# One-hot table reads: seven tables in the first half and ten in every later one, and a new order for the last tile, on one Trainium2 core

## The chip, the cores and the metric

The kernel runs on 1 core of one Trainium2 chip. The metric is the device time of one execution in microseconds; before the change the median of three runs is 620.69 us (620.36 to 627.76).

## The reference, cut to what matters

A batch of 2048 rows looks up 27 embedding tables of width 128, takes all pairwise dot products of the 27 rows of one sample, appends 16 dense features, and puts the 367 values through a small tower of layers.

```python
e = jnp.stack([tbl_f[ids[:, f]] for f in range(27)], axis=1)   # (2048, 27, 128); tables of 1000, 1250, 12500, 125000 rows
dot = jnp.einsum('bnd,bmd->bnm', e, e)
z = dot.reshape(2048, 27 * 27)[:, lower_triangle]              # 351 pairs
h = jnp.concatenate([z, dense_ctx], axis=1)                    # 367
h = jnp.maximum(h @ W_top1 + b_top1, 0.0)                      # 512
h = jnp.maximum(h @ W_top2 + b_top2, 0.0)                      # 256
y = h @ W_top3                                                 # 1
```

## The kernel before, in words

The batch is cut into 16 tiles (`t`) of 128 samples; two tiles make a half (`h`, eight of them). Every sample's 27 embedding rows must stand transposed in `embT` (the width of 128 on partitions). They get there in two ways.

**Gathered tables.** POOL issues one indirect DMA per table and tile (L324); it puts 128 rows of 512 bytes into `emb`, which holds two tiles. TensorE transposes them four at a time (a `quad`, L365), ScalarE copies the result to `embT` (L562). POOL may gather quad q of tile t+2 only when TensorE has transposed quad q of tile t (semaphore `turned`).

**Tables read by one-hot columns.** The small tables of `ONE_HOT` (1000 rows, 8 chunks of 125, or 1250 rows, 10 chunks) live in SBUF. VectorE builds a 125x256 one-hot block per chunk and half (`build`, L477), and TensorE multiplies the chunk by it (`read_table`): L355 with the table split in two parts, so two matmuls per chunk and 16 or 20 per read, or L350 on the unsplit table in the first half for tables 5 and up (8 per read; the trace has two records for each such plain fp32 matmul). ScalarE copies the result for both tiles at once (L554). Blocks are passed on in groups of two: TensorE waits for `hot_built`, and counts the used ones in `hot_used`, on which VectorE's builds (six groups ahead at most) and ScalarE's copies wait. Before the change, even halves read 9 tables so and gather 18 per tile; odd halves read 10 and gather 17.

**The rest of a tile.** `dots` (L381) makes the dot products of one tile in two steps of 64 small fp32 matmuls (128 records each), called first and second step here. VectorE transposes the result into `flat`, ScalarE picks the ring of pairs (`ring`, L570), TensorE transposes it (`flat`, L393) into `flatT`, and `layer1` (L410) and `layer2` (L434) follow one to three tiles later.

**What sets the order.** `plan(t)` writes the steps out by hand; each engine walks the same `ORDER`. In tile t it is: quad 0, first dots step of t-1, flat of t-2, a read; quad 1, a layer, a read; quad 2, second dots step, a layer, a read; quads 3 and 4, each with a read. The reads made during odd t are the first part of the next half's tables, those during even t the second part. Where only four reads fall to a tile (t = 3, 7, 11), the first place, between the first dots step and quad 1, has none. `END` holds what follows the last tile's quads. SyncE loads tables, ids and weights in program order (from L265); some tables are first put into space that a later tensor will use (`raw`).

## Time and profile before

| | |
|---|---|
| runs | 620.69 us median (620.36, 620.69, 627.76) |
| profiled execution | 628.72 us, span 626.9 us |
| TensorE busy, records | 423.8 us, 6065; mean granted clock 0.781 |
| VectorE busy | 246.2 us |
| ScalarE busy | 165.0 us |
| POOL busy (280 gathers) | 283.5 us |
| chain that ended last | PE 61%, issue 24%, unknown queue 8% |

The profiled execution is as long as the longest of the three runs, 8 us over the median. The span is what the trace covers; 1.8 us of the execution lie around it. Busy time of TensorE counts overlapping matmuls, so its share is not a share of its peak. POOL's gathers show how long it took to issue each, not when the rows landed. "remote" or "an unknown queue" in a wait means that what released it was not found beside a recorded instruction.

### The profile page before, as it was taken

The page shows a single profiled execution, that of the slowest core. Times are in us where ns is not written, and L with a number is a line of the kernel's source. Part 1 is how long each engine was busy: PE and PEld are TensorE (multiplying, and loading weights), DVE is VectorE, ACT ScalarE, POOL GpSimd, SP SyncE. Part 2 cuts the span into 40 slices and gives each one's busy share as a digit, 9 for nine tenths or more (in the row PEclk, how much of TensorE's full clock was granted, in tenths as well). Part 3 has the DMA queues.
Part 4 walks back from the last instruction along what each step waited for, and adds up shares of the span by engine and source line. Part 5 has one row for each costly group of instructions (what it writes and reads, how often), then busy time and mean ns, then how long its engine had stood idle before and what let it go on. Part 6 is the DMA issues. An engine that isn't in the chain of part 4 may idle for free.

```text
span 626.9 us, 13933 instructions
## 1 busy us (share of the span) xinstructions
PE 423.8 (68%) x6065; PEld 369.4 (59%) x6065; DVE 246.2 (39%) x760; ACT 165.0 (26%) x216; POOL 283.5 (45%) x288
## 2 busy tenths in 40 slices
PE   3206965656785693866578768486757777758997
PEld 3106765546675592855457657276645666638985
DVE  6107625527061361523416234162422524326622
ACT  2102232323222141221222213233121321214441
POOL 6774644544533476343643438534354533743000
PEclk9556966678776796777788669587767976959999
DMA  8932421514111122111212112111121211211000
GB/s 202 237 94 54 98 58 35 138 43 114 48 37 47 45 57 51 39 47 39 68 44 50 36 36 67 48 46 46 37 58 43 59 42 29 63 44 30 3 3 3
DMA packets 22924, 36.65 MB, mean 58 GB/s; under 512 B 6240, under 2 KB 17008, under 8 KB 22864
## 3 DMA queue, kind: packets, MB, share of 16 engines
q0 software_dynamic: 8960, 18.37, 11.8%
q1 hardware_dynamic: 13904, 17.39, 11.3%
q8 instruction: 48, 0.79, 0.5%
q14 instruction: 12, 0.10, 0.1%
HBM read 35.73 MB, written 0.01 MB: 57 GB/s over the span
## 4 chain that ended last, share of the span: by engine, by line
PE 61%; issue 24%; another core or an unknown queue 8%; ACT 3%; DVE 3%; DMA 1%; SPq 0%; ACTq 0%; DVEq 0%
PE embT_ps L355 23%; PE gram_ps L381 15%; PE h_ps L410 9%; PE h_ps L434 6%; PE embT_ps L365 4%; PE embT_ps L350 2%; PE flat_ps L393 2%; DVE one_hot L477 1%; ACT embT L554 1%; DVE tbl L462 1%; ACT embT L562 1%; DMA embT<-in_tbl 1%; ACT pairs L570 1%; ACT flatT L574 0%
## 5 line engine op out<-in xcount | busy, mean ns | idle before, releaser
L324 POOL DMA_INDIRECT emb<-in_tbl,idx x280 | 282.7, 1010 | 289.9 <-PE embT_ps L365 186.8
L477 DVE TENSOR_SCALAR one_hot<-ids,row_of 125x256 fp32r<-125x256 int32 x648 | 194.4, 368 | 204.7 <-PE embT_ps L355 119.9
L355 PE MATMUL embT_ps<-one_hot,tbl 125*128 125x256 f32 x1232 | 189.7, 312 | 45.0 <-issue 29.7
L355 PEld LDWEIGHTS embT_ps<-one_hot,tbl 125*128 125x128 f32 x1232 | 173.7, 213 | 50.3 <-issue 40.6
L381 PE MATMUL gram_ps<-embT 128*27 128x27 f32 x4096 | 98.7, 210 | 146.8 <-issue 128.9
L381 PEld LDWEIGHTS gram_ps<-embT 128*27 128x27 f32 x4096 | 71.2, 121 | 176.8 <-issue 156.9
L554 ACT COPY embT<-embT_ps 128x256 f32<-128x256 f32 x76 | 51.6, 682 | 278.7 <-PE embT_ps L355 176.1
L562 ACT COPY embT<-embT_ps 128x512 f32<-128x512 f32 (+2 forms) x80 | 88.6, 1110 | 11.5 <-remote 8.8
L508 DVE STREAM_TRANSPOSE flat<-gram_ps 128x864 f32<-128x864 f32 x16 | 17.3, 1083 | 123.1 <-PE gram_ps L381 123.1
L410 PE MATMUL h_ps<-flatT,w_sb 126*128 126x256 f32 (+1 forms) x192 | 56.0, 454 | 2.6 <-ACT flatT L574 2.5
L365 PE MATMUL embT_ps<-ident,emb 128*128 128x128 f32 x280 | 48.5, 293 | 3.6 <-issue 3.6
L410 PEld LDWEIGHTS h_ps<-flatT,w_sb 126*128 126x128 f32 x192 | 43.1, 242 | 11.6 <-ACT flatT L574 3.4
L365 PEld LDWEIGHTS embT_ps<-ident,emb 128*128 128x128 f32 x280 | 36.8, 152 | 4.9 <-issue 4.4
L434 PE MATMUL h_ps<-w_sb,h1T 128*128 128x256 f32 x128 | 39.3, 461 | 0.4 <-ACT h1T L594 0.2
L434 PEld LDWEIGHTS h_ps<-w_sb,h1T 128*128 128x128 f32 x128 | 28.4, 234 | 5.7 <-ACT h1T L594 0.5
L594 ACT ACTIVATE h1T<-h_ps 128x512 f32<-128x512 f32 x14 | 8.5, 607 | 81.5 <-PE h_ps L410 73.3
L574 ACT COPY flatT<-flat_ps 126x384 f32<-126x384 f32 x16 | 7.8, 485 | 58.9 <-PE flat_ps L393 52.4
L496 DVE TENSOR_TENSOR h<-h_ps,b_sb 128x256 f32<-128x256 f32 x16 | 6.8, 425 | 39.2 <-PE h_ps L434 39.2
L570 ACT COPY pairs<-flat 128x351 f32<-128x351 f32 x16 | 13.0, 813 | 2.7 <-DVE flat L509 2.7
L393 PE MATMUL flat_ps<-ident,pairs 128*126 128x128 f32 x48 | 11.9, 372 | 0.9 <-ACT pairs L570 0.9
L542 ACT CAST tbl<-embT 125x1024 fp32r<-125x1024 f32 (+1 forms) x5 | 5.7, 1133 | 15.1 <-DMA embT<-in_tbl 13.1
L509 DVE STREAM_TRANSPOSE flat<-gram_ps 128x416 f32<-128x416 f32 x16 | 9.2, 574 | 0.0
(39 smaller groups left out, 73.8 us busy)
## 6 DMA issues: line engine op xcount, KB each, us to landing
ids<-in_ids_hot SPq DMA_DIRECT2D x76, 128.0 KB
emb<-in_tbl,idx POOLq DMA_INDIRECT x280
embT<-in_tbl SPq DMA_DIRECT2D x3, 448.0 KB
embT<-in_tbl SPq DMA_DIRECT2D x2, 560.0 KB
w_sb<-in_tbl SPq DMA_DIRECT2D x2, 448.0 KB
w_sb<-in_W_ring SPq DMA_DIRECT2D x1, 756.0 KB
w_sb<-in_tbl SPq DMA_DIRECT2D x1, 560.0 KB
w_sb<-in_W_top SPq DMA_DIRECT2D x1, 512.0 KB
```

The source lines that it names most:

```text
L324: pool.indirect_dma_start(emb[:, t % EB, s, :], None, tables[f][:, :], bass.IndirectOffsetOnAxis(ap=idx[:, t, f:f + 1], axis=0),).then_inc ...
L355: mm = pe.matmul(out[:, 0:HN], tbl[0:ROWS, part, AT[o] + chunk, :], one_hot[0:ROWS, k % SLOTS, c, :], start=(chunk == 0 and part == 0), st ...
L365: mm = pe.transpose(out[:, i * P:(i + 1) * P], emb[:, t % EB, s, :], ident[:, :])
L381: mm = pe.matmul(gram_ps[32 * j:32 * j + FEATS, b, at * FEATS:(at + 1) * FEATS], rows, rows, start=True, stop=True)
L393: mm = pe.transpose(flat_ps[0:KR, k * TILE:(k + 1) * TILE], rows[:, k * KR:(k + 1) * KR], ident[:, :])
L410: mm = pe.matmul(h1_ps[:, i * width:(i + 1) * width], w1_sb[0:KR, k, c * P:(c + 1) * P], x[:, k, :], start=(k == 0), stop=(k == KC - 1))
L434: mm = pe.matmul(h2_ps[:, :], h1T[:, k, t % HT * TILE:(t % HT + 1) * TILE], w2_sb[:, k, :], start=(k == 0), stop=(k == C1 - 1))
L477: done = dve.tensor_scalar(one_hot[0:ROWS, k % SLOTS, c, :], of, row_of[0:ROWS, KINDS.index(CH[o]), chunk:chunk + 1], None, ALU.is_equal)
L508: dve.transpose(flat[:, 0:FEATS, :], by_column(0, FEATS)).then_inc(flat_filled, 1)
L554: act.copy(embT_feats[:, at:at + HT, slot(o), :], embT_ps[USE["hot", h, o] % BANKS][:, 0:HN].rearrange("p (t c) -> p t c", t=HT),).then_in ...
L562: act.copy(embT_feats[:, t % TB, s[0]:s[0] + n, :], embT_ps[USE["quad", t, q] % BANKS][:, 0:n * P].rearrange("p (f c) -> p f c", f=n),).th ...
L570: act.copy(pairs[:, t % 2, :, 1:HALF + 1], ring()).then_inc(pairs_ready, 1)
```

## The change

The one-hot tables are ordered so that the seven with 8 chunks come first. The first half (tiles 0 and 1) reads only those seven and gathers 20 tables per tile; all seven later halves read ten and gather 17. The three more rows gathered in tiles 0 and 1 than `emb` now has room for (17 per tile) land in `flatT`. The staging places of the unsplit tables and the order of SyncE's loads change with it: the last two tables are loaded in turn into `w1_sb` after the previous one there is split, and `flat` is no staging place any more. The last tile gets an order of its own. Counted over the program: 77 reads for 76, 1284 split matmuls for 1232, 16 unsplit for 32, 278 gathers for 280.

```diff
-ONE_HOT = (4, 13, 5, 6, 18, 19, 21, 22, 23, 8)
+ONE_HOT = (4, 13, 18, 19, 21, 22, 23, 5, 6, 8)
+READ_IN_HALF = (7, 10, 10, 10, 10, 10, 10, 10)
...
-    GF = FEATS - O
+    GF = FEATS - max(READ_IN_HALF)
...
     def hots_of(h):
-        return range(O if h % 2 else O - 1)
+        return range(READ_IN_HALF[h])
 
     def slot(o):
-        return GF if o == O - 1 else GF + 1 + o
+        return FEATS - 1 - o
...
         if t == T - 1:
-            after[QUADS - 2] += [("layer2", t - 3), ("ring", t - 1), ("flat", t - 1)]
-            after[QUADS - 1] += [("layer2", t - 2)]
+            return [("flat", t - 2), *dots[0], ("layer1", t - 3), ("quad", t, 0), *dots[2], ("layer1", t - 2),
+                    ("quad", t, 1), ("layer2", t - 3), ("quad", t, 2), ("ring", t - 1), ("flat", t - 1),
+                    ("layer2", t - 2), ("quad", t, 3), ("layer1", t - 1), ("quad", t, 4)]
...
-    END = [("dots", T - 1, 0, GROUPS32 // 2), ("layer1", T - 2), ("dots", T - 1, GROUPS32 // 2, GROUPS32),
-           ("layer2", T - 2), ("ring", T - 1), ("flat", T - 1), ("layer1", T - 1), ("layer2", T - 1)]
+    END = [("dots", T - 1, 0, GROUPS32), ("layer2", T - 2), ("ring", T - 1), ("flat", T - 1), ("layer1", T - 1),
+           ("layer2", T - 1)]
...
-    SPLIT_AT = {len(HOT0) + 1 + i: WHOLE + i for i in range(O - 1 - WHOLE)}
-    SPLIT_AT[len(HOT0) + O - 3] = O - 1
+    SHARED = WHOLE + 2
+    SPLIT_AT = {len(HOT0) + at: WHOLE + i for i, at in enumerate((0, 1, 2, 4, 6))}
...
-        emb = sb("emb", [P, EB, GF + 1, D])
+        emb = sb("emb", [P, EB, GF, D])
...
+        def gathered_row(t, s):
+            if s >= GF:
+                return flatT[:, s - GF, t * D:(t + 1) * D]
+            return emb[:, t % EB, s, :]
...
-                home = (flat, h1T, w2_sb, w1_sb, w1_sb)[o - WHOLE]
+                home = (h1T, w2_sb, w1_sb, w1_sb, w1_sb)[o - WHOLE]
...
-            for o in range(O - 1):
+            for o in range(SHARED + 1):
                 load_table(o)
-                load_ids(o)
+                if o < len(HOT0):
+                    load_ids(o)
...
             for n in range(EARLY, len(HOTS)):
                 load_ids(n)
-                if n == EARLY + 2:
-                    load_table(O - 1)
+                if n == EARLY:
+                    load_table(SHARED + 1)
+                elif n == EARLY + 2:
+                    load_table(SHARED + 2)
+                    sp.wait_ge(hot_used, BEFORE[len(HOT0)])
                     sp.dma_start(w2_sb[:, :, :], w2.rearrange("(k p) n -> p k n", p=P)).then_inc(weights_loaded, 16)
-                elif n == EARLY + 6:
+                elif n == EARLY + 5:
                     sp.wait_ge(low_ready, O)
                     sp.dma_start(w1_sb[0:KR, :, :], w1).then_inc(weights_loaded, 16)
...
                 dve.wait_ge(dotted, t + 1)
                 if t > 0:
                     dve.wait_ge(pairs_ready, t)
-                else:
-                    dve.wait_ge(low_ready, WHOLE + 1)
```

**TensorE's queue at the start** (line numbers moved: L355, L350, L365, L381 are L371, L366, L381, L397 after the change). Before, from the first read to the first dots step:

```order
L355 MATMUL embT_ps<-one_hot,tbl 128x256 x52
L365 MATMUL embT_ps<-ident,emb 128x128 x4
L355 MATMUL embT_ps<-one_hot,tbl 128x256 x20
...
L350 MATMUL embT_ps<-one_hot,w_sb 128x256 x16
L365 MATMUL embT_ps<-ident,emb 128x128 x6
L381 MATMUL gram_ps<-embT 27x27 x64
```

and now:

```order
L371 MATMUL embT_ps<-one_hot,tbl 128x256 x32
L381 MATMUL embT_ps<-ident,emb 128x128 x4
L371 MATMUL embT_ps<-one_hot,tbl 128x256 x16
...
L366 MATMUL embT_ps<-one_hot,w_sb 128x256 x8
L381 MATMUL embT_ps<-ident,emb 128x128
L381 MATMUL embT_ps<-ident,flatT 128x128 x3
L381 MATMUL embT_ps<-ident,emb 128x128 x4
L397 MATMUL gram_ps<-embT 27x27 x64
```

The first quad now stands after two reads, not three; two unsplit reads stand ahead of the first dots step, not four.

**TensorE's queue in tile 3**, from the first dots step to the second one, before:

```order
L381 MATMUL gram_ps<-embT 27x27 x64
L393 MATMUL flat_ps<-ident,pairs 126x128 x3
L365 MATMUL embT_ps<-ident,emb 128x128 x4
L410 MATMUL h_ps<-flatT,w_sb 128x256 x6
L355 MATMUL embT_ps<-one_hot,tbl 128x256 x16
L365 MATMUL embT_ps<-ident,emb 128x128 x4
```

and now:

```order
L397 MATMUL gram_ps<-embT 27x27 x64
L409 MATMUL flat_ps<-ident,pairs 126x128 x3
L371 MATMUL embT_ps<-one_hot,tbl 128x256 x16
L381 MATMUL embT_ps<-ident,emb 128x128 x4
L426 MATMUL h_ps<-flatT,w_sb 128x256 x6
L371 MATMUL embT_ps<-one_hot,tbl 128x256 x16
L381 MATMUL embT_ps<-ident,emb 128x128 x4
```

A read of 16 matmuls has come between the first dots step and quad 1. The same happens in tiles 7 and 11.

## Rows read from the trace of the kernel before

**Rows 1.** The page: each engine's busy time, share of the span, instructions.

```profile
PE 423.8 (68%) x6065; PEld 369.4 (59%) x6065; DVE 246.2 (39%) x760; ACT 165.0 (26%) x216; POOL 283.5 (45%) x288
```

**Rows 2.** Waits: engine line <- what it waited for: us in total, times, longest.

```profile
POOL emb L324 <- PE embT_ps L365: 186.8, 29, 10.9
PE gram_ps L381 <- issue: 128.9, 205, 1.9
ACT embT L554 <- remote: 87.7, 13, 30.3
PE embT_ps L365 <- issue: 3.6, 5, 1.6
```

**Rows 3.** Windows around single dots steps: length, busy us (instructions), clock, DMA.

```profile
461.10:467.30 6.20, 3.44 (x129) 2.42 (x129) 0.00 (x0) 1.62 (x2) 3.32 (x4) 0.50 0.16 42
494.30:504.90 10.60, 4.20 (x130) 2.77 (x129) 1.96 (x6) 2.31 (x3) 5.66 (x6) 0.75 0.24 63
227.00:228.20 1.20, 1.19 (x128) 1.16 (x128) 0.99 (x4) 1.20 (x2) 1.20 (x1) 1.00 0.15 44
583.80:585.00 1.20, 1.20 (x130) 1.13 (x128) 0.81 (x4) 1.20 (x2) 0.00 (x0) 1.00 0.00 0
```

**Rows 4.** Timeline, 0 to 54 us: start, us, engine line, [idle before <-releaser].

```profile
2.79 1.10 POOL L324 DMA_INDIRECT emb<-in_tbl,idx  x1 [1.15 <-DMA idx<-in_idx_rows]
12.43 2.63 PE L355 MATMUL embT_ps<-one_hot,tbl 125*128 125x256 f32 x16 [0.33 <-issue]
...
46.81 0.95 POOL L324 DMA_INDIRECT emb<-in_tbl,idx  x1 [0.30 <-issue]
47.99 0.61 DVE L477 TENSOR_SCALAR one_hot<-ids,row_of 125x256 fp32r<-125x256 int32 x2 [10.58 <-remote]
...
53.60 1.18 ACT L554 COPY embT<-embT_ps 128x256 f32<-128x256 f32 x2 [30.26 <-remote]
54.19 0.94 POOL L324 DMA_INDIRECT emb<-in_tbl,idx  x1 [6.44 <-remote]
```

**Rows 5.** Timeline, 54 to 86 us.

```profile
69.23 7.07 PE L350 MATMUL embT_ps<-one_hot,w_sb 125*128 125x256 f32 x32
...
83.25 0.94 POOL L324 DMA_INDIRECT emb<-in_tbl,idx  x1 [0.30 <-issue]
...
85.35 0.98 PE L381 MATMUL gram_ps<-embT 128*27 128x27 f32 x61 [1.14 <-issue]
```

**Rows 6.** Windows, tiles 7 to 10, each from its quad 0 to the next.

```profile
302.60:340.50 37.90, 25.77 (x374) 22.33 (x373) 13.34 (x42) 9.70 (x13) 17.17 (x19) 0.77 0.19 48
340.50:379.80 39.30, 27.72 (x376) 23.98 (x374) 14.78 (x51) 9.52 (x13) 17.18 (x15) 0.74 0.17 43
379.80:419.10 39.30, 27.25 (x391) 23.62 (x390) 14.73 (x47) 10.49 (x14) 21.01 (x21) 0.78 0.20 52
419.10:456.20 37.10, 26.19 (x378) 22.35 (x377) 15.23 (x49) 9.04 (x12) 16.21 (x18) 0.82 0.19 48
```

**Rows 7.** Timeline, TensorE: the read between first dots step and quad 1.

```profile
505.42 3.76 PE L355 MATMUL embT_ps<-one_hot,tbl 125*128 125x256 f32 x16
508.98 1.06 PE L365 MATMUL embT_ps<-ident,emb 128*128 128x128 f32 x4
...
228.51 2.16 PE L355 MATMUL embT_ps<-one_hot,tbl 125*128 125x256 f32 x16
230.51 0.60 PE L365 MATMUL embT_ps<-ident,emb 128*128 128x128 f32 x4
```

**Rows 8.** Timeline at 220 us, and POOL's gathers in the view by line (min/median/max).

```profile
220.55 7.45 DVE L477 TENSOR_SCALAR one_hot<-ids,row_of 125x256 fp32r<-125x256 int32 x28
222.42 6.39 POOL L324 DMA_INDIRECT emb<-in_tbl,idx  x1 [9.24 <-PE embT_ps L365]
...
L324 POOL DMA_INDIRECT emb<-in_tbl,idx x280: 938/944/6390, 2.8 to 573.3; - x140
```

**Rows 9.** Windows, quad 0 of tile 15 to the end.

```profile
594.00:626.90 32.90, 27.45 (x642) 22.97 (x640) 7.00 (x19) 11.24 (x17) 0.00 (x0) 0.99 0.01 3
```

## What the change is expected to do

> **What bounds the kernel now.** I read the page first: TensorE is busy for 423.8 us of 626.9 and no engine is full [rows 1], so the bound is a chain between engines. The waits come next [rows 2]. TensorE hardly ever waits for gathered rows (3.6 us before the transposes), but POOL waits 186.8 us for the transposes that free its buffers. The largest idle time of TensorE, 128.9 us in 205 pieces, lies inside the dots steps and has no releaser ("issue"). So I looked at single dots steps [rows 3]. All have the same 128 records. Where POOL issues nothing, at 583.8, a step takes 1.2 us; with about five gathers it takes 6.2 us, with about seven 10.6 us. The step at 227.0 tells the two causes apart that one could think of: POOL is counted busy there, but by one gather that is itself stuck (below), and the step takes 1.2 us. TensorE is therefore held while gathers are being issued, and let go some 2.8 us after the last one starts (83.25 to 86.1 in [rows 5]; the last record of that step starts within the row at 85.35).
>
> The same is seen, much larger, at the start [rows 4]. POOL issues the 36 gathers of tiles 0 and 1 without a pause, from 2.79 to 46.81, 1.25 us apart (0.94 busy and 0.30 idle). The 16 matmuls of the second table begin at 12.43, yet ScalarE's copy that waits for them starts at 53.60, and VectorE's builds that wait for `hot_used` come ten microseconds apart. All are released together 5.8 us after POOL's last gather of the burst ends (47.76), and POOL itself goes on at 54.19.
>
> So I read the kernel as turns. TensorE passes quads, which lets POOL gather 4 to 10 rows in one burst; the next dots step ends 2.8 us after that burst; only then does TensorE go on to the quad that starts the next burst. There are two such turns in a tile of 37 to 39 us [rows 6]. Two things are on the path: each gather, at 1.25 us, and what TensorE does between the end of a dots step and the next quad. Reads elsewhere lie beside the gathers. The last 32.9 us have no gather [rows 9].
>
> **The Trainium skill against this.** The rows show dots steps of 6 to 10 us beside gathers and 1.2 us without. The Trainium skill, page "SBUF — State Buffer", section "Who interferes with whom", says that TensorE and ScalarE never wait for anyone at SBUF. By that page alone the gathers would cost TensorE nothing; what follows from it is the first rival.
>
> **The change, part by part** (against the profiled execution, 628.72 us).
>
> *1. Four more gathers in tiles 0 and 1, three fewer reads there.* The first burst is 40 gathers for 36: its last one starts at 46.81 + 4 x 1.25 = 51.8, and by the same lag the release moves from 53.60 to 58.6 and POOL's restart from 54.19 to 59.2 [rows 4]. Before the first dots step can end, POOL issues 21 more (17 of tile 2, 4 of tile 3). Before, these took from 54.19 to 83.25, 29.1 us, of which 20 x 1.25 = 25.0 are gathers and 4.1 are pauses in which POOL waited for quads. TensorE has less to do in this stretch now: two of four unsplit reads go, each a half of the 7.07 us that the last two took [rows 5]. That can take away pauses, no more. The last gather then starts between 59.2 + 25.0 = 84.2 and 88.3, for 83.25: +1.0 to +5.1. I take +2.0, near the lower end, since the quads now come sooner after one another. The lower bound, if the hold is not tied to the gathers, is -7.1 (the two reads). Both ends are kept for the range. That three rows go to `flatT` costs nothing: it is first written by tile 0's ScalarE copy, after quad 4 of both tiles.
>
> *2. A read between the first dots step and quad 1 in tiles 3, 7 and 11.* This place had none, and it is on the path. The same read stands there in tile 12, from 505.42 to 508.98 (3.56 us), and in tile 5, from 228.51 to 230.51 (2.00 us) [rows 7]; the former ran at the low level of the granted clock, the latter at the high one. I take the mean, 2.8: 3 x 2.8 = +8.4 (6.0 to 10.7).
>
> *3. Chunk counts by place.* With the 10-chunk tables last, the read between second dots step and quad 3 has 20 matmuls in even tiles and 16 in odd ones. Against before that is four more matmuls in each of the seven even tiles from 2 to 14, and four fewer in tiles 1, 5, 9 and 13. A matmul there is 2.00/16 to 3.56/16, 0.12 to 0.22 us [rows 7], so four are 0.6, and three times four more make +1.8. The other reads grow too (52 split matmuls more in all), beside gathers: nothing while that cover holds, up to 4 us if it does not.
>
> *4. Six gathers fewer,* one each for tiles 4, 5, 8, 9, 12, 13: 6 x 1.25 = -7.5, all on the path. If they are not, nothing.
>
> *5. The last tile.* Every gather starts by 573.3 [rows 8], 20 us before tile 15 begins at 594.0 [rows 9]. Its last quad has waited for no gather, so putting older work ahead of it hides nothing. The same matmuls run in another order. What is lost is cover: layer2 of tile 13 stood between quad 4 and the dots of tile 15, and TensorE now waits there for one ScalarE copy: +0.5.
>
> *6. SyncE.* The last two tables are now loaded behind waits on `low_ready`, with the ids of later reads queued behind them. Those ids are six reads ahead of their use, about a tile or more, and layer1 first needs the weights near 162 us. I cost both at nothing; if that cover is gone, one late table holds ScalarE's copies for some microseconds, once.
>
> The sum is 2.0 + 8.4 + 1.8 - 7.5 + 0.5 = +5.2: 633.9 us by the profiled execution. That execution is 8.0 us above the median of the runs shown, so against the median it is 620.7 + 5.2 = 625.9; I predict **626**.
>
> **The rivals.** *Gathers do not hold TensorE.* The six fewer save nothing and the four more cost nothing; what counts is matmuls: 52 split ones more at 0.12 to 0.22 us (+6 to +11) and 32 unsplit records fewer (-7.1). The steps of 1.2 us with an idle POOL speak against it. It gives 620 to 625. By the page named above this would be the result.
>
> *The first release comes sooner.* The hold to 53.60 could follow the table traffic or the number of reads rather than the length of the burst. For: the delays there are far longer than in any later burst. Against: VectorE was still held at 47.99, at the burst's end. Then part 1 is -7.1 instead of +2.0: 616.8.
>
> *POOL is locked out less often.* At 222.42 one gather takes 6.39 us, against a median of 0.944, and ends 0.8 us after VectorE's 28 builds without a gap (220.55 to 228.0) have ended [rows 8]. It happens three times, in tiles 4, 8 and 12. Its price: tile 8 with it against tile 10 is 39.3 - 37.1, plus 1.25 for a gather fewer, 3.4; tile 9 after it against tile 7 is 1.4, where a read and a gather fewer make 1.55, so -0.1 [rows 6]. Together 3.3 each. If the shifted order ends all three: -9.9, or 616.0. The Trainium skill (same page and section) has VectorE and GpSimd exclude each other only where a VectorE instruction uses two ports or two SBUF inputs; the builds read one SBUF tensor and take 266 ns for 256 elements, no doubled rate, so by the page there would be no lock and nothing to gain; the 6.39 us gather speaks against it.
>
> *POOL is locked out more often: slower.* In even tiles three reads of 10 chunks now stand in a row, so VectorE's builds after quad 3 run longer without a gap, just where POOL restarts. Today the lock comes in three of the seven even tiles from 2 to 14. If it came in all seven, 4 x 3.3 = 13.2 more: 639.1. It decides from three more on (635.8).
>
> **Chances and range.** The forecast 0.45; no hold 0.12; sooner release 0.12; fewer lockouts 0.16; more lockouts 0.15. Two per cent, 12.4 us, is about what a measurement of this kernel can tell from no change: 608.3 and 633.1 are the edges. Below 608.3 the time comes only if a sooner release and fewer lockouts meet: 0.10. Above 633.1 lie the more-lockouts case and the upper end of the forecast's parts 1 and 2 (+5.1, +10.7): 0.17. The rest, 0.73, is within. The range 609 to 638 takes in the faster rivals whole and the slower one to just below its full size, and leaves about 0.1 on each side. The forecast's own range, by the bounds of parts 1 and 2, is 619 to 633.
>
> **What would show it.** Right: POOL's first burst is 40 gathers and the first copy by ScalarE after it starts near 58.6; the first dots step ends near 88; tiles 3, 7, 11 are some 1.5 us longer than tile 7 was, tiles 6 and 10 about 0.7 shorter (a gather less, four matmuls more); the last 33 us are unchanged. Wrong: dots steps that stay at 6 to 10 us beside an idle POOL; a release well before 58; a number of gathers over 6 us other than three, or a gather that the quads of the last two tiles wait for.

## The result

| | median | runs |
|---|---|---|
| before | 625.76 us | 20 (620.36 to 629.67) |
| changed | 628.42 us | 20 (623.52 to 630.99) |

The ratio is 1.0052, 95% interval 1.0026 to 1.0077: half a per cent slower, no change by the bound of 2 per cent. The forecast was 626.0 us, or +5.2 us; measured are 628.42 us, and 0.52% of 625.76, which is +3.3 us. The kernel before took 5.1 us more in these 20 runs than in the three that the forecast started from, so that the nearness of 628.42 to 626 owes something to luck. The profiled execution of the changed kernel took 626.05 us with a span of 624.2. The one of before (span 626.9) was a long one for its kernel, so the two spans hide the difference; I compare stretches, and leave the size of the change to the timed runs.

### The profile page after: what moved, and what is told of

It reads as the page before. It is cut to its first block, busy times and chain, and to the rows that moved or that the text cites. A ratio compares the mean times of both kernels' runs of the same rounds, so it can differ in the third digit from the quotient of the medians.

```text
span 624.2 us, 13981 instructions
## 1 busy us (share of the span) xinstructions
PE 412.1 (66%) x6083; PEld 357.5 (57%) x6083; DVE 245.8 (39%) x770; ACT 164.4 (26%) x217; POOL 307.0 (49%) x286
## 4 chain that ended last, share of the span: by engine, by line
PE 61%; issue 25%; another core or an unknown queue 8%; ACT 2%; DMA 2%; DVE 1%; POOL 0%; ACTq 0%; DVEq 0%
PE embT_ps L371 26%; PE gram_ps L397 14%; PE h_ps L426 8%; PE h_ps L450 5%; PE embT_ps L381 5%; PE flat_ps L409 2%; DMA emb<-in_tbl,idx 2%; ACT embT L567 1%; DVE one_hot L493 1%; ACT pairs L583 1%; POOL emb L340 0%; PE embT_ps L366 0%; ACT embT L575 0%; DMA idx<-in_idx_rows 0%
## 5 line engine op out<-in xcount | busy, mean ns | idle before, releaser
L340 POOL DMA_INDIRECT emb<-in_tbl,idx x272 | 300.4, 1105 | 256.6 <-PE embT_ps L381 157.4
L371 PE MATMUL embT_ps<-one_hot,tbl 125*128 125x256 f32 x1284 | 194.1, 308 | 43.9 <-DVE one_hot L493 18.9
L371 PEld LDWEIGHTS embT_ps<-one_hot,tbl 125*128 125x128 f32 x1284 | 177.8, 209 | 49.6 <-issue 26.4
L397 PE MATMUL gram_ps<-embT 128*27 128x27 f32 x4096 | 93.4, 207 | 132.1 <-issue 126.1
L397 PEld LDWEIGHTS gram_ps<-embT 128*27 128x27 f32 x4096 | 67.6, 118 | 160.6 <-issue 152.2
L575 ACT COPY embT<-embT_ps 128x512 f32<-128x512 f32 (+1 forms) x80 | 88.6, 1110 | 20.1 <-remote 16.5
L381 PE MATMUL embT_ps<-ident,emb 128*128 128x128 f32 x272 | 47.8, 289 | 21.1 <-ACT embT L567 11.5
L426 PE MATMUL h_ps<-flatT,w_sb 126*128 126x256 f32 (+1 forms) x192 | 50.7, 421 | 6.4 <-issue 6.4
L381 PEld LDWEIGHTS embT_ps<-ident,emb 128*128 128x128 f32 x272 | 34.0, 148 | 24.8 <-issue 22.9
L426 PEld LDWEIGHTS h_ps<-flatT,w_sb 126*128 126x128 f32 x192 | 39.4, 222 | 13.9 <-issue 7.6
L478 DVE TENSOR_TENSOR tbl<-w_sb,tbl 125x1280 fp32r<-125x1280 f32 (+1 forms) x4 | 5.7, 1422 | 11.4 <-issue 7.3
L409 PEld LDWEIGHTS flat_ps<-ident,pairs 128*126 128x126 f32 x48 | 6.1, 166 | 6.6 <-ACT pairs L583 4.6
## 6 DMA issues: line engine op xcount, KB each, us to landing
w_sb<-in_W_top SPq DMA_DIRECT2D x1, 512.0 KB
```

Source lines behind the costliest of these rows:

```text
L340: pool.indirect_dma_start(gathered_row(t, s), None, tables[f][:, :], bass.IndirectOffsetOnAxis(ap=idx[:, t, f:f + 1], axis=0),).then_inc(g ...
L371: mm = pe.matmul(out[:, 0:HN], tbl[0:ROWS, part, AT[o] + chunk, :], one_hot[0:ROWS, k % SLOTS, c, :], start=(chunk == 0 and part == 0), st ...
L381: mm = pe.transpose(out[:, i * P:(i + 1) * P], gathered_row(t, s), ident[:, :])
L397: mm = pe.matmul(gram_ps[32 * j:32 * j + FEATS, b, at * FEATS:(at + 1) * FEATS], rows, rows, start=True, stop=True)
L409: mm = pe.transpose(flat_ps[0:KR, k * TILE:(k + 1) * TILE], rows[:, k * KR:(k + 1) * KR], ident[:, :])
L426: mm = pe.matmul(h1_ps[:, i * width:(i + 1) * width], w1_sb[0:KR, k, c * P:(c + 1) * P], x[:, k, :], start=(k == 0), stop=(k == KC - 1))
```

## The profile after

The page of the changed kernel, beside [rows 1], and its waits, beside [rows 2]:

```profile
PE 412.1 (66%) x6083; PEld 357.5 (57%) x6083; DVE 245.8 (39%) x770; ACT 164.4 (26%) x217; POOL 307.0 (49%) x286
```

```profile
ACT embT L567 <- PE embT_ps L371: 206.2, 54, 20.6
POOL emb L340 <- PE embT_ps L381: 157.4, 22, 9.4
PE gram_ps L397 <- issue: 126.1, 193, 2.2
ACT embT L567 <- remote: 49.0, 12, 15.4
```

POOL issues two gathers fewer and is counted busy 23.5 us more; its waits for the transposes fall by 29.4. The pauses inside the dots steps stay (128.9, now 126.1). So the picture is that of before, but POOL has more long gathers.

**The start**, timeline of the changed kernel, 16 to 91 us, beside [rows 4, 5]:

```profile
16.18 0.66 PE L381 MATMUL embT_ps<-ident,emb 128*128 128x128 f32 x4 [1.30 <-DMA emb<-in_tbl,idx]
...
40.16 1.09 PE L381 MATMUL embT_ps<-ident,emb 128*128 128x128 f32 x4 [10.55 <-ACT embT L567]
...
63.62 0.94 POOL L340 DMA_INDIRECT emb<-in_tbl,idx  x1 [0.30 <-issue]
70.94 0.67 ACT L567 COPY embT<-embT_ps 128x256 f32<-128x256 f32 x1 [20.63 <-PE embT_ps L371]
71.24 0.94 POOL L340 DMA_INDIRECT emb<-in_tbl,idx  x1 [6.67 <-remote]
...
84.42 0.57 PE L397 MATMUL gram_ps<-embT 128*27 128x27 f32 x45 [2.67 <-ACT embT L575]
```

The first burst is not 40 gathers, as I had it, but 48: two quads of tile 0 are turned early (the first at 16.18), so POOL goes on into tile 2 without a pause. ScalarE's copy is released at 70.94, not at 58.6. It is again some six microseconds after the burst's end (64.56). A third quad of tile 0 stands in the trace at 40.16, and it is all that POOL needs for its next four gathers; POOL goes on only at 71.24. So during a burst not only TensorE's matmuls come late but also the news that they are done. The first dots step ends at 90.7; it was 86.3 before. Most of this delay is made up soon: quad 0 of tile 2 comes at 116.45 us, and came at 115.09.

**The middle**, windows of single dots steps, beside [rows 3], and of tiles 7 to 10, beside [rows 6] (columns as there):

```profile
377.30:379.20 1.90, 1.39 (x129) 1.25 (x129) 0.91 (x4) 1.76 (x3) 1.73 (x1) 1.00 0.14 49
391.00:403.20 12.20, 4.40 (x130) 3.06 (x128) 1.22 (x4) 2.98 (x4) 7.49 (x8) 0.55 0.23 55
414.10:423.90 9.80, 3.76 (x129) 2.48 (x128) 1.37 (x5) 2.38 (x3) 5.36 (x6) 0.78 0.28 67
431.90:440.60 8.70, 3.08 (x130) 2.42 (x129) 1.62 (x6) 1.44 (x2) 4.72 (x5) 0.77 0.29 62
```

```profile
301.70:338.70 37.00, 26.13 (x382) 21.59 (x380) 13.53 (x45) 10.17 (x14) 20.57 (x21) 0.82 0.22 54
338.70:376.80 38.10, 26.79 (x387) 23.37 (x385) 16.23 (x56) 9.07 (x13) 18.02 (x15) 0.82 0.17 45
376.80:413.90 37.10, 25.72 (x382) 21.68 (x381) 13.89 (x45) 9.98 (x14) 20.27 (x21) 0.82 0.21 53
413.90:451.90 38.00, 26.34 (x387) 23.27 (x385) 16.13 (x55) 9.07 (x13) 17.96 (x15) 0.82 0.19 44
```

These four tiles took 153.6 us [rows 6] and take 150.2. I had forecast +0.9 for them (one read more, a few matmuls, two gathers fewer). Taken as pairs from quad 0 to quad 0, tiles 6 and 7, where the read was added, took 74.9 us and take 75.0; tiles 8 and 9, whose reads are as many as before, took 78.6 and take 75.2. The granted clock of the four windows was 0.77, 0.74, 0.78 and 0.82; it is 0.82 in each now. Whether the higher clock is a cause of the shorter tiles or follows from them, no run separates.

**The lock-out.** The timeline at 220 us and the view by line, beside [rows 8]:

```profile
219.55 8.50 DVE L493 TENSOR_SCALAR one_hot<-ids,row_of 125x256 fp32r<-125x256 int32 x32
221.81 7.05 POOL L340 DMA_INDIRECT emb<-in_tbl,idx  x1 [9.17 <-PE embT_ps L381]
227.26 1.24 PE L397 MATMUL gram_ps<-embT 128*27 128x27 f32 x125 [0.38 <-ACT embT L567]
...
L340 POOL DMA_INDIRECT emb<-in_tbl,idx x272: 938/944/7064, 2.8 to 565.3; - x136
```

A gather of 6.7 to 7.1 us now comes in every even tile from 2 to 12, six times for three. While POOL is stuck in it, the next dots step runs free: 1.24 us for 125 records.

**The last tile**, TensorE's timeline. First the kernel before, then the changed one:

```profile
609.43 1.27 PE L381 MATMUL gram_ps<-embT 128*27 128x27 f32 x128
613.51 1.12 PE L381 MATMUL gram_ps<-embT 128*27 128x27 f32 x111
614.87 0.32 PE L381 MATMUL gram_ps<-embT 128*27 128x27 f32 x17 [0.24 <-issue]
```

```profile
587.53 0.55 PE L409 MATMUL flat_ps<-ident,pairs 128*126 128x128 f32 x3 [1.35 <-ACT pairs L583]
...
601.40 0.55 PE L409 MATMUL flat_ps<-ident,pairs 128*126 128x128 f32 x3 [1.79 <-ACT pairs L583]
...
607.79 2.04 PE L397 MATMUL gram_ps<-embT 128*27 128x27 f32 x221 [0.88 <-ACT embT L575]
612.03 0.48 PE L397 MATMUL gram_ps<-embT 128*27 128x27 f32 x35 [2.20 <-issue]
```

And the windows from the last read to the end, before and after:

```profile
591.20:626.90 35.70, 30.25 (x666) 25.77 (x664) 8.52 (x25) 12.28 (x19) 0.00 (x0) 0.99 0.01 3
```

```profile
583.50:624.20 40.70, 29.95 (x666) 25.70 (x664) 8.13 (x24) 12.34 (x19) 0.00 (x0) 1.00 0.01 2
```

The same 666 records at the same clock, no more busy time, and 5.0 us more: all of it idle. Four new waits make 6.2 us (1.35, 1.79, 0.88, 2.20); before, the waits in their places were 0.36 and 0.24.

## The experiments

The theory I went in with: TensorE is held while POOL issues gathers; a gather is on the path; the new last tile costs more than I gave it. The main rival: the dots steps are long for other reasons, and only the number of matmuls counts. A second question: what does a lock-out cost?

Ratios are to the kernel before, timed on the same chip, with 95% intervals. Three chips ran the experiments. On two of them the kernel before takes 622 to 624 us, near the 625.76 of the first measurement. On the third it takes 383.5 us (381.4 to 385.0, 17 runs); I call it **the quick chip**.

### One: the last tile alone, and the rest without it

after_oldtail is the changed kernel with this undone, before_newtail the kernel before with this alone:

```diff
+            return [("flat", t - 2), *dots[0], ("layer1", t - 3), ("quad", t, 0), *dots[2], ("layer1", t - 2),
+                    ("quad", t, 1), ("layer2", t - 3), ("quad", t, 2), ("ring", t - 1), ("flat", t - 1),
+                    ("layer2", t - 2), ("quad", t, 3), ("layer1", t - 1), ("quad", t, 4)]
...
-    END = [("dots", T - 1, 0, GROUPS32 // 2), ("layer1", T - 2), ("dots", T - 1, GROUPS32 // 2, GROUPS32),
-           ("layer2", T - 2), ("ring", T - 1), ("flat", T - 1), ("layer1", T - 1), ("layer2", T - 1)]
+    END = [("dots", T - 1, 0, GROUPS32), ("layer2", T - 2), ("ring", T - 1), ("flat", T - 1), ("layer1", T - 1),
+           ("layer2", T - 1)]
```

> The changed kernel with the last tile's order and END as they were before. Theory (the new order of the last tile loses cover and costs about 5 us, as the two traces show): about 5 us under the changed kernel's 628, so 623, ratio to before 0.997, and the time from the last read's first matmul to the end of the span back from 40.7 to some 35.7 us. Rival (the last tile's order is worth 0.5 us at most, as I predicted, and the longer end in the trace is one execution's): 628, ratio 1.004.

> The kernel before with only the last tile's new order and the new END. Theory: the end grows by about 5 us, ratio to before 1.008, 631 us. Rival (order of the end is worth 0.5 us): ratio 1.001.

Measured: after_oldtail 623.92 us, ratio 1.0011 (0.9977 to 1.0044); before_newtail 629.57, ratio 1.012 (1.007 to 1.017), against 623.51. The new last tile costs about 7 us put on the kernel before, and taking it off the changed kernel gives back some 3 to 6 us. In the traces the stretch from quad 0 of tile 14 to the end is 54.5 us before and 55.7 in after_oldtail, against 59.5 in before_newtail and 60.5 in the changed kernel.

A second trace of the changed kernel (after_copy, experiment five) has 63.2 us there. Of the difference, 2.4 us lie behind the first record of the last dots step: after the pause in that step the granted clock fell to 0.50, and the same matmuls took longer. First the line of the changed kernel, then that of after_copy with its window:

```profile
616.15 1.60 PE L437 MATMUL h_ps<-flatT,w_sb 126*128 126x128 f32 x12 [0.57 <-ACT flatT L587]
```

```profile
618.80 2.93 PE L437 MATMUL h_ps<-flatT,w_sb 126*128 126x128 f32 x12 [0.57 <-ACT flatT L587]
615.90:622.60 6.70, 6.13 (x25) 5.00 (x25) 1.47 (x6) 1.65 (x3) 0.00 (x0) 0.50 0.01 2
```

So a part of what the new last tile costs comes in some executions only.

### Two: ten reads alone, and the changed kernel with nine

```diff
-        return range(O if h % 2 else O - 1)
+        return range(O if h else O - 1)
```

```diff
-READ_IN_HALF = (7, 10, 10, 10, 10, 10, 10, 10)
+READ_IN_HALF = (7, 10, 9, 10, 9, 10, 9, 10)
```

> The kernel before with ten tables read in halves 2, 4 and 6 too (and 17 gathers there); first half, table order, loads and end as before. By the terms of the prediction (a read of 16 on the path three times, 8.4 us, against six gathers at 1.25) it is 2 to 3 us slower, ratio 1.004. By what the trace of the changed kernel shows for tiles 2 to 13 (9.8 us less than before) it is up to 10 us faster, ratio 0.985.

> The changed kernel with nine tables read in halves 2, 4 and 6 (18 gathers per tile there), the rest as changed: new start, new chunk order, new end. If ten reads in all halves are what made the middle shorter, this is about 10 us over the changed kernel (638, ratio 1.02). By the prediction's terms it is 2 to 3 us under it (626, ratio 1.00).

Measured: before_ten 618.45 us, ratio 0.9942 (0.9909 to 0.9975); after_nine 632.54, ratio 1.0171 (1.0113 to 1.0228). Three more reads for six gathers fewer are worth 3.6 us in the kernel before, and 4 to 7 in the changed one (1.0171 against 1.0114 and 1.0052, other comparisons). before_ten beats both kernels. It differs from after_oldtail in the first half, the order of the tables and SyncE's loads: 1.0011/0.9942 is 4.3 us; the two intervals together leave roughly 1.4 to 7.2. The traces do not put all of this at the start: quad 0 of tile 2 comes at 115.70 and 116.35 us, 0.65 apart, and from there to quad 0 of tile 14 it is 447.2 and 450.4 us.

### Three: fewer gathers, plain DMAs, on the quick chip

Both leave something out. after_quarter issues only the first gather of each quad from tile 2 on, so most rows are stale; after_plain fetches the first 128 rows of each table with plain DMAs from ScalarE's queue, not the rows looked up. In this order:

```diff
-                    for s in quad(t, q):
+                    for s in issued(t, q):
...
+        return quad(t, q) if t < EB else quad(t, q)[:1]
```

```diff
-            for t in range(T):
+            for t in range(EB):
...
+                if t + EB < T:
+                    for r in quad(t + EB, q):
+                        act.dma_start(emb[:, t % EB, r, :], tables[GATHERED[r]][0:P, :]).then_inc(plain[t % EB][q], 16)
```

> The changed kernel with only the first gather of each quad issued from tile 2 on: 110 gathers instead of 278, the other rows of a quad are stale, so three quarters of the gathered values are left out. Matmuls, copies and reads are all there. Theory (while POOL issues gathers, the small matmuls of the dots steps are held; a gather in a burst costs 1.25 us on the path): the dots steps of tiles 3 to 13, 6 to 12 us now, shrink to 1.1 to 3 us and a tile falls from 37.5 to some 26 us or less (twelve to thirteen gathers x 1.25 = 16 us less, of which some is then bound by reads): 450 to 520 us. Rival (gathers do not hold TensorE; the steps are long because of the matmuls themselves, the weight loads or the granted clock): steps stay at 6 to 12 us and the time stays within 2 per cent of the changed kernel, 616 to 640 us.

> The changed kernel with the rows of tiles 2 to 15 fetched by plain DMAs of 128 rows each, issued on ScalarE's queue right after its wait for the transposes; the rows are the first 128 of each table and not the looked-up ones, so the lookup is left out while bytes, places and order stay the same. POOL issues only the 40 gathers of tiles 0 and 1. Theory A (it is POOL's work of issuing an indirect gather that holds TensorE, not the rows that land): dots steps of 1.1 to 3 us though the same 64 KB per table still land; tiles near 26 us, total 450 to 520 us, unless ScalarE's issuing becomes the bound. Theory B (the row traffic into SBUF holds TensorE): dots steps stay at 6 to 12 us and the total at 600 us or more.

Measured: 369.0 us, ratio 0.9613 (0.9575 to 0.965), and 379.6, ratio 0.9889 (0.9839 to 0.9939), against 383.5. This decides nothing on the hold, since the quick chip hardly has it. There a dots step beside gathers takes 1.6 to 1.9 us. Windows of after_end, below, and its wait of POOL, which takes the place of 157.4 us:

```profile
259.20:261.10 1.90, 1.78 (x129) 1.53 (x130) 1.90 (x7) 1.64 (x2) 1.45 (x2) 1.00 0.44 107
268.80:270.50 1.70, 1.61 (x130) 1.38 (x129) 0.00 (x0) 1.38 (x2) 1.40 (x2) 1.00 0.63 102
```

```profile
POOL emb L340 <- PE embT_ps L381: 2.8, 9, 0.3
```

Gathers are issued at the same pace there (0.94 us each, 1.25 apart), and a tile takes 21 us instead of 37.5. On that chip the premise of my first rival holds: gathers hardly hold TensorE.

### Four: the same with plain DMAs where gathers hold TensorE

> The same kernel as after_plain (rows of tiles 2 to 15 by plain DMAs on ScalarE's queue, the lookup left out), because that one ran on a chip where the kernel before takes 383.5 us and where the dots steps take 1.6 us beside gathers. Meant for a chip where the kernel before takes about 620 us. There, theory A (POOL's issuing of indirect gathers holds TensorE): dots steps of 1.1 to 3 us, a total of 400 to 480 us, near what the other chip gives. Theory B (the row traffic holds it): steps of 6 to 12 us and 600 us or more. Theory C (that chip holds TensorE's instructions and semaphores beside any DMA): steps between, also in the last tiles. If this run too falls on a chip of the 383.5 us kind, it must give 378 to 382 us and tells nothing new.

Measured in one execution, where the kernel before takes 622.22 us: **409.8 us**. The page, and a window around a dots step:

```profile
PE 329.0 (81%) x6083; PEld 305.0 (75%) x6083; DVE 233.2 (57%) x770; ACT 166.9 (41%) x217; POOL 40.6 (10%) x48
```

```profile
245.00:246.30 1.30, 1.21 (x129) 1.17 (x129) 0.12 (x1) 0.62 (x2) 0.00 (x0) 1.00 0.38 108
```

The rows still land, at 108 GB/s in this window, and the step takes 1.2 us. So what holds TensorE is the gathers issued by POOL, not rows that land (theory A). Whether it is POOL's own work or what an indirect DMA does elsewhere, the runs do not separate. The ten tiles from quad 0 of tile 4 to that of tile 14 take 211.7 us here and 211.4 on the quick chip: without gathers the chips are alike. Nearly all of the 30 us that are left between them (409.8 and 379.6) lie in the start, where both still issue 40 gathers: quad 0 of tile 2 comes at 93.1 against 64.1. From quad 0 of tile 2 to that of tile 14, 204 gathers fewer save 449.6 - 257.4 = 192.2 us against the changed kernel (after_copy, below): 0.94 us for each, on average and with whatever bounds the kernel next.

### Five: what a lock-out costs

```diff
+                    if k > 0:
+                        dve.wait_ge(hot_built, k)
                     for c in range(GROUP):
```

> The changed kernel with one wait more per group of one-hot builds on VectorE (it waits until its own previous group is finished), which leaves a small gap between groups, so that POOL is not shut out by a long unbroken row of builds. Theory of the prediction (each lock-out costs 3.3 us): the six gathers of 6.7 to 7.1 us fall under 2 us and the kernel gains 6 x 3.3 = 20 us, 608 us, at least 10. Rival (a lock-out only shifts POOL's burst: TensorE's next dots step runs free in 1.1 to 1.7 us meanwhile, and the two-tile period with a lock-out, 75.1, is the one without): the long gathers vanish and the time stays within 3 us of the changed kernel, or rises, since the gaps delay the builds by some 0.1 us per group, 640 groups.

> The same kernel as after_gap, meant for a chip where the kernel before takes about 620 us. Theory of the prediction (each lock-out of POOL costs 3.3 us): no gather over 3 us from tile 2 on, and 10 to 20 us less than the changed kernel in the same comparison. Rival (a lock-out only shifts POOL's burst, and TensorE runs free meanwhile): the long gathers vanish, the dots step that took 1.1 to 1.9 us in every even tile takes 6 us or more again, and the time is the changed kernel's within 4 us, or up to 8 us more, as on the other chip (392.1 against 384).

> The changed kernel as it is, beside the kernel before on the same chip. On a chip where the kernel before takes about 620 us: 0 to 5 us slower, as first measured, 1.000 to 1.008. On a chip where it takes 383.5 us, TensorE never waits for a burst and POOL is counted busy to the end: there the extra reads are on the path and the six gathers fewer are not, which is the prediction's first rival, and the last tile costs its 5 us in full: 386 to 392 us, 1.005 to 1.02. If the last tile's order is all that counts there, it equals after_end within 2 us.

Measured on the quick chip: after_gap 392.1 us, ratio 1.0206 (1.0167 to 1.0244), so the waits only cost time there (after_end, experiment six, has 384.4 us). On a chip of the first kind: gap_again 627.63, ratio 1.0086 (1.0056 to 1.0117), after_copy 629.26, ratio 1.0114 (1.0049 to 1.0178), against 622.22. The two intervals overlap, so the gap gains nothing that these runs can tell. gap_again's gathers by line, and two dots steps (the first was the free one):

```profile
L340 POOL DMA_INDIRECT emb<-in_tbl,idx x272 | 262.9, 967 | 292.0 <-PE embT_ps L381 205.3 <-issue 69.2 <-remote 16.4
```

```profile
377.80:383.90 6.10, 3.06 (x128) 2.19 (x128) 1.45 (x5) 1.65 (x2) 3.45 (x4) 0.67 0.25 65
392.90:400.70 7.80, 2.75 (x130) 2.35 (x128) 0.00 (x0) 1.51 (x2) 3.93 (x5) 0.76 0.27 62
```

The long gathers are gone: POOL's busy time falls from 300.4 to 262.9 us, and its wait rises from 157.4 to 205.3. The free step is gone too (6.1 us for 1.9) and the step after it is shorter (7.8 for 12.2). Even and odd tiles take 39.4 and 35.7 us instead of 38.0 and 37.1: 75.1 for two, either way. A lock-out costs nothing in this order; the rival is right. In the order of before it was not tried.

### Six: the last dots in two steps again

```diff
-    END = [("dots", T - 1, 0, GROUPS32), ("layer2", T - 2), ("ring", T - 1), ...
+    END = [("dots", T - 1, 0, GROUPS32 // 2), ("layer2", T - 2), ("dots", T - 1, GROUPS32 // 2, GROUPS32), ...
```

> The changed kernel with only one thing of the new end undone: the dots of the last tile in two steps again, with layer2 of tile 14 between them instead of behind them. Theory (128 small matmuls in a row run out of supply: the 2.20 us pause with no releaser before the last 35 records of that step): the pause falls to 0.3 us or less and the time by 1.5 to 2.5 us. Rival (the 2.20 us pause comes from something else, such as a fetch of instructions at a fixed distance, or the layer2 matmuls placed between cost as much as they hide): the pause moves or stays, and the time changes by less than 1 us.

Measured on the quick chip: 384.36 us, ratio 1.0018 (0.9995 to 1.0042) to the kernel before; the changed kernel itself was not timed there, so the gain in time stays open. Its TensorE timeline:

```profile
365.50 1.27 PE L397 MATMUL gram_ps<-embT 128*27 128x27 f32 x128 [0.88 <-ACT embT L575]
366.70 2.00 PE L450 MATMUL h_ps<-w_sb,h1T 128*128 128x256 f32 x8
368.63 0.91 PE L397 MATMUL gram_ps<-embT 128*27 128x27 f32 x84
369.73 0.56 PE L397 MATMUL gram_ps<-embT 128*27 128x27 f32 x44 [0.19 <-issue]
372.79 0.55 PE L409 MATMUL flat_ps<-ident,pairs 128*126 128x128 f32 x3 [2.50 <-ACT pairs L583]
373.90 2.47 PE L437 MATMUL h_ps<-flatT,w_sb 126*128 126x128 f32 x12 [0.57 <-ACT flatT L587]
```

The pause of 2.2 us has become one of 0.19. Every execution with the long step has it, 2.03 to 2.38 us, on both kinds of chip: after 221 records in the changed kernel and its kin, after 239 in before_newtail, after 148 in after_nine.

Its place stays where it was in the program. Counted in matmul records from the end, the pause stands before the 79th in all seven traces of the changed kernel's last tile, and the 0.19 us of after_end before the 80th. In before_newtail the 2.37 us stand before the 61st, and so do the 0.24 us of the kernel before. So the program sets where it falls, as the rival had it, and its size goes with what stands ahead of that place: 2.0 us or more in a long row of small matmuls, 0.2 when the row is broken by larger ones. Single steps of 128 records can have such a pause too, with no gather near: 0.43 us in after_oldtail, 0.61 in before_ten. What it is stays open.

The layer2 that stood behind the dots no longer hides ScalarE's copy: the wait before the `flat` step is 2.50 us. From the first dots record to the end it takes 18.1 us; in the changed kernel 16.4 (607.79 to 624.2), and in after_gap, on the quick chip too, 16.4. Of the 1.7 us between them the clock accounts for all: it was granted at 0.51 from 374.4 to 377.8 us, and the two halves of layer1 took 2.47 and 2.31 us for 1.60 and 1.50. Without that the two ends are alike: what was saved is given back, and nothing is gained.

### Seven: the dots steps where POOL stands still

Experiment four says that only a dots step beside gathers is slow. In the order of before, each stands right behind a quad, the very thing that sets POOL off. ten_dots is before_ten with them moved:

```diff
+            late = 0 < t < T - 1
+            if late and q in (1, 2):
+                out += dots[2 * q - 2]
             out.append(("quad", t, q))
-            out += dots[q] if q < len(dots) else []
+            if not late:
+                out += dots[q] if q < len(dots) else []
```

> The kernel of before_ten (618.45 us, the old start and the old last tile, ten reads from the second half on) with one thing moved: in tiles 1 to 14 the first dots step stands in front of quad 1 and the second in front of quad 2, instead of right behind quad 0 and quad 2. Matmuls, gathers and copies are the same. Theory (TensorE is starved of instructions only while POOL issues gathers, and the dots steps, 256 short instructions each, suffer most; four of them take 31.8 of the 75.1 us of two tiles): in front of a quad POOL has issued most of what it may and stands still, so the steps fall from 6 to 10 us to 1.1 to 5 us, two tiles take 10 to 20 us less, and the total is 480 to 560 us. Rival (POOL and TensorE take turns whatever the order: a later quad frees the buffers later, and POOL's bursts move behind it by as much): the steps get shorter but POOL's waits grow, two tiles stay at 72 to 78 us, and the total is 600 to 640 us. On a chip where the kernel before takes 383.5 us neither applies, and the time is within 2 per cent of it, 376 to 390 us.

Measured: **508.24 us** (505.15 to 512.0, 6 runs), ratio 0.8152 (0.8114 to 0.8189), against 623.14. Four dots steps that follow one another, of before_ten and then of ten_dots:

```profile
450.40:451.60 1.20, 1.20 (x128) 1.16 (x129) 1.20 (x5) 1.20 (x2) 1.20 (x1) 1.00 0.22 56
459.30:475.80 16.50, 4.38 (x130) 2.87 (x128) 1.05 (x4) 1.83 (x2) 9.49 (x10) 0.61 0.18 52
488.30:497.60 9.30, 3.64 (x129) 2.47 (x128) 1.52 (x5) 2.29 (x3) 4.90 (x6) 0.78 0.29 65
505.80:514.50 8.70, 3.22 (x130) 2.29 (x129) 1.06 (x4) 1.47 (x2) 4.73 (x5) 0.78 0.23 60
```

```profile
227.50:229.20 1.70, 1.70 (x129) 1.59 (x128) 0.00 (x0) 0.67 (x1) 0.00 (x0) 0.50 0.56 55
233.40:237.00 3.60, 2.16 (x130) 1.71 (x128) 1.60 (x5) 0.67 (x1) 1.18 (x2) 0.86 0.25 66
256.40:258.60 2.20, 1.62 (x130) 1.38 (x130) 0.67 (x3) 0.67 (x1) 0.35 (x1) 0.98 0.43 93
263.60:266.00 2.40, 1.47 (x130) 1.41 (x129) 0.66 (x2) 0.66 (x1) 0.55 (x1) 1.00 0.31 83
```

POOL's column shows the cause: 9.49, 4.90 and 4.73 us of gathers beside a step have become 0 to 1.18. And the waits of ten_dots:

```profile
POOL emb L328 <- PE embT_ps L369: 92.7, 40, 3.5
PE gram_ps L385 <- issue: 30.4, 55, 1.2
```

In before_ten they are 182.9 and 146.4 us. Two tiles take 57 us for 75. The same gathers, matmuls and copies in another order: the turns overlap. The mean granted clock is 0.875 for 0.798, so a part of the gain comes through the clock; how much is not separated.

## Why the prediction was right, and where it was not

**In short.** The total came out by luck. Of the signs that I had named for being right, none came: the first burst was 48 gathers for 40, the first copy came at 70.9 us for 58.6, the first dots step ended at 90.7 for "near 88", tile 7 became 0.9 us shorter and not 1.5 longer, tiles 6 and 10 became 0.9 us longer and not 0.7 shorter, and the end grew by 5 us. Of the signs for being wrong, the other number of long gathers came.

**The hold by gathers: right, and it carried the argument.** Experiments four and seven show it. What I could not know is that it belongs to the chip: the quick one hardly has it, and there the premise of the rival *gathers do not hold TensorE*, chance 0.12, holds. The Trainium skill, page "SBUF — State Buffer", section "Who interferes with whom", says that TensorE never waits for others at SBUF. The runs do not contradict this sentence: with the rows landing and no gathers the steps took 1.2 us. They show that it does not cover this loss, whose pauses end on "issue".

**Term 1, the start (+2.0, bounds -7.1 to +5.1): sign right, size open.** At the end of the first dots step the loss is 4.3 us in the trace (90.66 for 86.33), but at quad 0 of tile 2 it is 1.4 (116.45 for 115.09); in five traces of the new start that quad comes at 115.4 to 116.5 us, in the three of the old one at 114.7 to 115.7. The timed runs of experiments one and two give 4.3 us, with the order of the tables and the loads in it. I took the burst for 40 gathers because only tiles 0 and 1 have room; that two quads are turned early enough for eight more I did not see. The lag after the burst held.

**Terms 2, 3 and 4, the middle (+8.4, +1.8, -7.5): the sum +2.7 is wrong.** before_ten has the reads and gathers of it and measured -3.6 us (-5.7 to -1.6). From quad 0 of tile 2 to that of tile 14, two traces of the order of before take 457.3 and 451.6 us (before, before_newtail); four with ten reads take 447.2 to 450.4 (before_ten, after, after_copy, after_oldtail). On average that is 5.9 us less.

Term 2 failed, and it is half of the miss. I costed the read by its own length, as if the quad behind it would come later by as much. It does not: in tile 7, quad 1 comes 11.99 us after quad 0 in the kernel before, without the read, and 11.91 us after it in gap_again, with the read and with no gather locked out. What gave way is a wait: before the dots step of tile 7 TensorE waited 4.55 us for ScalarE in the kernel before, behind a burst that is one gather longer, and 1.71 us in gap_again. In the changed kernel POOL is locked out just then, the wait is 0.37 us, the step takes 1.3 us for 6.2, and quad 1 comes after 4.94 us; but the second step of that tile then takes 12.4 us for 7.9.

This is a reading of traces. No run moved the read alone, so how the six to nine microseconds by which the middle came out quicker divide between the read, the gathers and the granted clock (0.82 in all four tiles, from 0.74 to 0.82 before) stays open. Pairs of tiles say where the miss lies. By my terms a pair with the added read (6 and 7, 10 and 11) should have grown by 2.2 us (2.8 + 0.6 - 1.25) and the pair behind it (8 and 9, 12 and 13) shrunk by 1.25, for the gather less at its start. In the two traces the former stayed as they were, within 0.2 us, and the latter fell by 3.4 and 3.5 us (from 78.6 and 78.7 to 75.2 and 75.1). So half of the miss, about two microseconds a pair, stands where the read was added, and half where none was; for the second half I have the clock and the lock-outs as candidates, and no experiment. Term 4 is of the right order: 0.94 us a gather by experiment four, where I had 1.25.

**Lock-outs.** "A number of gathers over 6 us other than three" came true, six, and it costs nothing by experiment five. My 3.3 us came from comparing tile 8, at whose end POOL is locked out, with tile 10. But by quad 3 tile 8 was already 2.8 us behind (34.79 and 31.99 us after quad 0), and its lock-out begins only at 35.7. What made it longer came earlier: a first dots step of 10.59 us for 9.55, beside one gather more, and reads and transposes at the lower granted clock (the first read 3.76 us for 3.06; 0.74 for 0.82 in [rows 6]).

**Term 5, the last tile (+0.5): far too small.** 5.0 us in the traces, 3 to 7 by experiment one, with up to 2.4 us of it from the clock in single executions. I looked for the cover of one ScalarE copy and found it; there were three, and a pause of 2.20 us in the long step. That nothing could be gained there was right.

**Term 6, SyncE (0)**: no wait for ids or weights stands among the waits after.

By the runs the parts are -3.6, +4.3 and 3 to 7, together 4 to 8, for 3.3 measured first and about 7 (ratio 1.0114) the second time. The total was right because two errors cancelled: the middle was forecast some 6 us too slow, start and end together 5 to 9 us too quick.

One bound of the prediction does not follow from its terms. With +5.1 and +10.7 the sum is +10.6, which is 631.3 us; it gave 633, and counted this end among the cases above 633.1. At the other end +1.0 and +6.0 give 622.5 us, and -7.1 with +6.0 gives 614.4; 619 is neither.

## What to carry to other kernels

Where a trace shows an engine held during another's bursts, ask first what stands beside the burst: moving many short instructions away from it gave 18 per cent here, while trading gathers for matmuls gave half a per cent. A step put where its engine already waits need not cost its length, and single tiles of a pattern that repeats after several are poor prices: look at the idle time of the place, and at the granted clock, over a whole period before adding it up. In a tail without slack, write down every wait that the old order covered.

## What the runs showed of the hardware

- Two kinds of chip: 622 to 626 us and 383.5 us for the same kernel. The mean granted clock differs with it (0.78 to 0.81, and 0.973 in after_end), but not as the cause alone: with plain DMAs (0.941) the first kind gives 211.7 us for ten tiles, the quick chip (0.973) 211.4.
- Beside gathers, TensorE's small matmuls come in groups of some five records with pauses of 0.4 or 1.1 us ended by "issue". Whether this is the supply of instructions was not tried; why one chip shows it and another does not stays open. TensorE's signals come late as well: a quad recorded at 40.16 us releases POOL at 71.24.
- A step of 256 records pauses once for 2.0 to 2.4 us, with no gather near, on both kinds of chip; in two steps of 128 with other matmuls between them the pause is 0.2 us, at the same place of the program (79 and 80 records from its end, 61 in before and before_newtail).
- In the last tile the granted clock fell to 0.5 behind a pause or a wait in some executions (after_copy, after_end), and the same twelve matmuls took 2.9 and 2.5 us for 1.6.
- Rows of VectorE builds without a gap keep a POOL gather for 6.3 to 7.2 us (7.18 in after_nine); a wait between groups of two ends this (967 ns on average instead of 1105), at no gain.
